# The lower left quarter of a symmetric score matrix from block transposes on VectorE and DMA

## The reference

```
h = layernorm(x) * (1 + ca) + sa              # per batch, 1024 x 256
scores = (h * w_lhs) @ (h * w_rhs).T          # 1024 x 1024
x = x + ga * (softmax(scores, axis=-1) @ h)
h = layernorm(x) * (1 + cb) + sb
x = x + gb * (relu(h @ W1 + b1) @ W2 + b2)    # 256 -> 1024 -> 256
```

## Time and profile before

| | us |
|---|---|
| median of three runs | 720.35 |
| the profiled execution, whole | 725.38 |
| its span | 723.5 |
| TensorE busy | 708.4 (98%) |
| VectorE busy | 562.3 (78%) |
| ScalarE busy | 404.5 (56%) |
| GpSimd busy | 353.8 (49%) |

### The profile page before, as it was taken

How to read it: one execution, slowest core, us unless ns; L and a number is a source line. 1 busy time by engine, 2 the same in 40 slices (tenths; PEclk the granted TensorE clock), 3 DMA queues, 4 the chain that set the end, 5 groups by cost and what they waited for, 6 DMA issues and landing times.

```text
span 723.5 us, 13394 instructions
## 1 busy us (share of the span) xinstructions
PE 708.4 (98%) x4711; PEld 647.2 (89%) x4711; DVE 562.3 (78%) x1041; ACT 404.5 (56%) x565; POOL 353.8 (49%) x394
## 2 busy tenths in 40 slices
PE   8989899999999999999999999999999999999997
PEld 7667789998999989999899989999899998999996
DVE  3578788888889888897898887898888974886521
ACT  2244319842587427872586715874278725665462
POOL 3363336462665245562564526752455624235543
PEclk8889999999999999999999999999999999999999
DMA  8022342213611253122432225112531222011300
GB/s 291 24 82 68 108 117 88 95 59 108 166 49 59 88 170 91 58 84 81 125 87 87 79 78 169 50 58 87 160 101 58 80 84 91 1 37 59 94 32 30
DMA packets 52288, 63.92 MB, mean 88 GB/s; under 512 B 4576, under 2 KB 46624, under 8 KB 52256
## 3 DMA queue, kind: packets, MB, share of 16 engines
q1 hardware_dynamic: 52256, 63.50, 28.7%
HBM read 39.34 MB, written 24.15 MB: 88 GB/s over the span
## 4 chain that ended last, share of the span: by engine, by line
PE 88%; DVE 2%; POOL 0%; issue 0%; DVEq 0%
PE acc L481 8%; PE col L536 8%; PE col L538 8%; PE acc L482 8%; PE col L537 8%; PE acc L487 8%; PE score L597 7%; PE score L600 7%; PE score L596 7%; PE score L521 4%; PE score L522 4%; PE score L523 4%; PE score L527 3%; PE score L579 1%; POOL ln_t L916 0%; DVE score L771 0%
## 5 line engine op out<-in xcount | busy, mean ns | idle before, releaser
L925 POOL TENSOR_TENSOR hid_lo<-hid,hid_hi 128x512 fp32r<-128x512 f32 x128 | 170.4, 1333 | 246.1 <-ACT hid_hi L625 245.3
L621 ACT ACTIVATE hid<-col,b1T 128x512 f32<-128x512 f32 x128 | 87.1, 680 | 113.0 <-PE col L538 107.1
L481 PE MATMUL acc<-W2hi,hid_hi 128*128 128x256 f32 x512 | 127.2, 282 | 0.0
L482 PE MATMUL acc<-W2lo,hid_hi 128*128 128x256 f32 x512 | 125.7, 279 | 0.0
L597 PE MATMUL score<-V,Phi 128*128 128x256 f32 x448 | 109.8, 283 | 0.0
L596 PE MATMUL score<-V,Phi 128*128 128x258 f32 x448 | 109.6, 280 | 0.0
L625 ACT ACTIVATE hid_hi<-hid 128x512 fp32r<-128x512 f32 x128 | 81.0, 633 | 49.2 <-PE acc L487 45.3
L749 DVE TENSOR_SCALAR_CACHE_REDUCE S<-score 128x1024 f32<-128x1024 f32 x64 | 78.0, 1220 | 33.9 <-PE score L527 29.8
L536 PE MATMUL col<-h2hi,W1hi 128*128 128x512 f32 x256 | 103.0, 402 | 0.2 <-DVE h2lo L848 0.2
L538 PE MATMUL col<-h2hi,W1lo 128*128 128x512 f32 x256 | 101.0, 394 | 0.0
L537 PE MATMUL col<-h2lo,W1hi 128*128 128x512 f32 x256 | 100.6, 393 | 0.0
(11 more groups left out here) (106 smaller groups left out, 1366.9 us busy)
## 6 DMA issues: line engine op xcount, KB each, us to landing
block_rows<-blocks SPq DMA_DIRECT2D x30, 512.0 KB, 2.9
blocks<-block_rows SPq DMA_DIRECT2D x120, 128.0 KB, 3.0
x_cur<-x SPq DMA_DIRECT2D x16, 512.0 KB, 3.9
ln_t<-x SPq DMA_DIRECT2D x14, 512.0 KB, 4.8
out<-x_mlp SPq DMA_DIRECT2D x8, 512.0 KB, 3.0
out<-x_mlp SPq DMA_DIRECT2D x16, 256.0 KB, 2.2
W_sb<-W SPq DMA_DIRECT2D x2, 1024.0 KB, 10.1
attn_mod<-mod_rows SPq DMA_DIRECT2D x8, 256.0 KB, 3.5
```

Of the source, the lines that this page charges most:

```text
L481: nc.tensor.matmul(o, hi, W2hi[:, it, :], start=(it == 0 and t % 2 == 0), stop=False, skip_group_check=True)
L482: nc.tensor.matmul(o, hi, W2lo[:, it, :], start=False, stop=False, skip_group_check=True)
L621: nc.scalar.activation(hid[:, n % 2, :], col[n % 2][:], ACT.Relu, bias=b1T[:, n % FT:n % FT + 1]).then_inc(col_read, 1)
L925: G.tensor_tensor(hid_lo[:, n % RING, :], hid[:, n % 2, :], hid_hi[:, n % RING, :].bitcast(F32), ALU.subtract).then_inc(hid_lo_done, 1)
```

## The change

For batches 1 to 7 TensorE no longer makes the lower left quarter (rows 512 to 1023, columns 0 to 511) of the scores. Batch 0 is computed as before.

- SC.4 to SC.7 compute, transpose and copy the right 512 columns only. Of their 4, 5, 6 and 6 transposes 0, 1, 2 and 2 are left.
- ST.0 to ST.3, new on VectorE: the right half of row tile n (128x512) is transposed in 32x32 blocks into `stage`.
- SW.0 and SW.1, new on SyncE's queue: each stores two tiles of `stage` (512 KB) to DRAM. SR.0 and SR.1 load them back in four DMAs of 128 KB each, with the blocks in their new places, into `lower`. `stage` and `lower` lie over the rings `Phi` and `Plo`.
- SB.0 to SB.3 become two subtractions of 512 columns, from `S` and from `lower`.
- MX.0, new on VectorE: the maximum over `lower` (128x2048) per row tile, and a maximum of four columns with `row_max`.
- MB is split: MB.0 (four transposes) can run when row tile 3 is read, MB.1 waits for MX.
- Waits: ScalarE's SM.1 waits until `stage` is stored, VectorE's SM.1 and SM.2 until `lower` is read.
- All lists are in another order. Of those only the loop's start on SyncE is shown in the diff.

```diff
-        AM.0 GA.0- S2.1- XT.0+ X1.0 GB.0 R2.1- SH.0+ XT.1+ RH.0+ O0.0- SH.1+ RH.1+ S2.0 R2.0 X0.0+ O1.0-
+        AM.0 GA.0- S2.1- X1.0 XT.0+ SW.0 R2.1- SR.0 SW.1 SR.1 SH.0+ XT.1+ RH.0+ GB.0 SH.1+ O0.0- RH.1+ S2.0
...
+                    elif kind == "SW":
+                        sp.wait_ge(stage_done, HT * (b - 1) + 2 * n + 2)
+                        sp.dma_start(score_blocks[n], stage[:, n].rearrange("p u v t r -> p (u v t r)")).then_inc(stage_stored, 16)
+                    elif kind == "SR":
+                        sp.wait_ge(stage_stored, 16 * (2 * b + n - 1))
+                        for u in range(Q):
+                            sp.dma_start(lower[u * QP:(u + 1) * QP, n].rearrange("a u v t r -> a u (v t r)"),
+                                         score_blocks[n][:, u * 2 * P:(u + 1) * 2 * P].rearrange("(u a) f -> a u f", a=QP)).then_inc(scores_turned, 16)
...
-                        for lo_col in range(0, ROWS, HR):
+                        left = 0 if n < HT or ph is PH["first"] else HR
+                        for lo_col in range(left, ROWS, HR):
...
-                        for i in range(at // P):
+                        for i in range(left // P, at // P):
...
+                        if ph is PH["first"] or n == 1:
+                            pe.wait_ge(scores_read, T * b + T)
+                        else:
+                            pe.wait_ge(scores_read, T * b + HT)
+                        if ph is not PH["first"] and n == 1:
+                            pe.wait_ge(max_ready, b)
+                        for j in range(n * HT, (n + 1) * HT):
...
-                        V_.tensor_scalar(S[:, n, :], score[n % 2][:], 1.0, None, ALU.mult, ALU.max,
+                        cols = slice(0 if n < HT or ph is PH["first"] else HR, ROWS)
+                        V_.tensor_scalar(S[:, n, cols], score[n % 2][:, cols], 1.0, None, ALU.mult, ALU.max,
...
+                        V_.tensor_tensor(tile[:, 0:HT], tile[:, 0:HT], most.broadcast_to([P, HT, P]), ALU.subtract)
+                        dve.wait_ge(scores_turned, 16 * Q * (2 * b + n // 2 - 1))
+                        V_.tensor_tensor(by_quarter(tile[:, HT:T]), lower[:, n // 2, :, :, n % 2, :].rearrange("p u v r -> p v u r"),
+                                         by_quarter(most.broadcast_to([P, HT, P])), ALU.subtract).then_inc(sub_done, 1)
+                    elif kind == "ST":
+                        dve.wait_ge(scores_read, T * b + n + 1)
+                        V_.transpose(stage[:, n // 2, :, :, n % 2, :], S[:, n, HR:ROWS].rearrange("p (v u r) -> p u v r", v=HT, r=QP)).then_inc(stage_done, 1)
+                    elif kind == "MX":
+                        wait_apart(dve, scores_turned, 16 * Q * 2 * b)
+                        V_.tensor_reduce(left_max[:], lower[:].rearrange("p h u v t r -> p v (h u) (t r)"), AX.XY, ALU.max).then_inc(left_done, 1)
+                        wait_apart(dve, scores_read, T * b + T)
+                        dve.wait_ge(left_done, b)
+                        V_.tensor_tensor(row_max[:, HT:T], row_max[:, HT:T], left_max[:], ALU.max).then_inc(max_ready, 1)
```

More of the change, by code:

```diff
@@ L9 @@
 ACT = mybir.ActivationFunctionType
+AX = mybir.AxisListType
 P = 128
@@ L229, in block_kernel @@
     mod_rows = nc.dram_tensor("mod_rows", [NB, 4, D], F32, kind="Internal").ap()
+    score_blocks = nc.dram_tensor("score_blocks", [2, P, Q * 2 * P], F32, kind="Internal").ap()
     block_rows = nc.dram_tensor("block_rows", [P, D * HT], F32, kind="Internal").ap()
@@ L250, in block_kernel @@
         with nc.sbuf_tensor("W1_sb", [P, DK, FF], F32) as W1_sb, nc.sbuf_tensor("W2_sb", [P, FT, D], F32) as W2_sb:
+            pass
+        with nc.sbuf_tensor("stage", [P, 2, Q, HT, 2, QP], F32) as stage, nc.sbuf_tensor("between", [P, 2, T, P], F32), \
+                nc.sbuf_tensor("lower", [P, 2, Q, HT, 2, QP], F32) as lower:
             pass
@@ L575, in part @@
                     elif kind == "MB":
-                        pe.wait_ge(scores_read, T * b + T)
-                        for j in range(T):
+                        if ph is PH["first"] or n == 1:
[5 more added lines that the diff above has]
+                        for j in range(n * HT, (n + 1) * HT):
                             last = nc.tensor.transpose(max_ps[:, j * P:(j + 1) * P], row_max[:, j:j + 1].broadcast_to([P, P]), ident[:])
-                            if j % HT == HT - 1:
-                                last.then_inc(max_done, 1)
+                        last.then_inc(max_done, 1)
                     elif kind == "AV":
@@ L755, in part @@
                             dve.wait_ge(max_done, 2 * b + n // HT + 1)
-                        most = max_ps[:, n * P:(n + 1) * P].unsqueeze(1).broadcast_to([P, T, P])
-                        V_.tensor_tensor(tile, tile, most, ALU.subtract).then_inc(sub_done, 1)
+                        most = max_ps[:, n * P:(n + 1) * P].unsqueeze(1)
+                        if ph is PH["first"] or n >= HT:
+                            V_.tensor_tensor(tile, tile, most.broadcast_to([P, T, P]), ALU.subtract).then_inc(sub_done, 1)
+                            continue
+                        V_.tensor_tensor(tile[:, 0:HT], tile[:, 0:HT], most.broadcast_to([P, HT, P]), ALU.subtract)
+                        dve.wait_ge(scores_turned, 16 * Q * (2 * b + n // 2 - 1))
+                        by_quarter = lambda ap: ap.rearrange("p v (u r) -> p v u r", u=Q)
+                        V_.tensor_tensor(by_quarter(tile[:, HT:T]), lower[:, n // 2, :, :, n % 2, :].rearrange("p u v r -> p v u r"),
[9 more added lines that the diff above has]
+                        V_.tensor_tensor(row_max[:, HT:T], row_max[:, HT:T], left_max[:], ALU.max).then_inc(max_ready, 1)
                     elif kind == "SM":
+                        if n in (1, 2):
+                            wait_apart(dve, left_done, b)
+                            wait_apart(dve, sub_done, T * b + 2 * n)
                         dve.wait_ge(phi_done, T * (b - 1) + n + 1)
```

99 lines of the change are left out of this document (51 added, 48 removed).

## The result

The changed kernel takes 728.68 us (median of 4 runs, 727.33 to 730.62) where the kernel before, in the same session, takes 720.49: the ratio is 1.0118, with a 95% interval of 1.0092 to 1.0145. The forecast was 710.0 with a range of 706.5 to 717, so it missed in sign. The profiled execution took 729.4 us, with a span of 727.6.

The account below looks back on a forecast made before the run. TensorE was taken to bound the kernel from 82 to 718 us. Median before 720.35, less 12.3 for transposes, plus 0.8 in batch 0, plus 0.15 a batch for small waits, gave 709.9, rounded to 710; range 706.5 to 717.

Parts of the forecast that it names:

- place 1: At the loop's edge, AV.3 to F.0: VectorE needs 20.1 us, TensorE's work 21.0, leaving 0.9 us spare.
- The first rival: VectorE late at the loop's edge, 0.5 to 1.1 us a batch: 712.5 to 717; chance 0.30 including a dear reduction.
- The clause on the port: VectorE and GpSimd share a port, locked by VectorE's two-SBUF-input reads; added instructions with one such input lengthen nothing.
- The transposes: 112 left out of SC.4 to SC.7 in seven batches, 0.110 us each: 12.3 us off TensorE, the ceiling.
- the prices of the added work: VectorE's ST, MX and split SB less halved copies: +2.95 us a batch, 72.5 to 75.4; MX at 2.2.
- bounds of +1.7 and +5.4: Lower and upper limit in us of the work a batch added to VectorE, put at +2.95.
- Place 2: Scores' trip through DRAM after ST.1: 8.0 us, covered by 8.4 us of VectorE work; MB.1 about 6 to spare; cost 0.
- place 3: Row tile 5, SC.6's last transposes behind L1.0's wait for `ln_t`: half a microsecond at most against 0.8 spare; cost 0.
- slower rival: DMA trip holds VectorE at SB.0; over 1.3 us of wait is its sign; 13 us trip ends at 733; chance 0.04.
- The tail: After the last batch, a reordering behind a TensorE that has no gap: 0 us.
- the 0.15 for small waits: Waits shorter than could be resolved, 0.15 us a batch, seven times, added to the sum.
- Batch 0: AV.4 is read later on VectorE, so batch 1's F.0 starts at 82.9: +0.8 us, bounds -0.5 and +2.5.

Follow-up runs that it names:

- e3: Changed kernel with the output store O0.0 ahead of SH.1 on SyncE's queue in the loop: 721.44 us.
- e4: Changed kernel with B2.0 behind XG.1 and SM.6 on VectorE in the loop: 722.91 us.
- e5: Changed kernel with GpSimd's three adds of attn_mod (XC.1 to XC.3) moved ahead in the loop's list: 725.34 us.
- e1: Kernel before, with TensorE leaving out the 16 left transposes of SC.4 to SC.7 in batches 1 to 7; result not computed: 710.97 us.
- e8: Changed kernel with the output store ahead of SH.1 and B2.0 behind XG.1 and SM.6, GpSimd's list untouched: 717.40 us.
- e12: As e8, with MB.1 in batch 1 moved on TensorE from behind F.7 to behind F.8: 714.96 us.
- e6: Changed kernel with output store ahead of SH.1, B2.0 behind XG.1 and SM.6, and GpSimd's adds early: 721.18 us.
- e2: Changed kernel with its lists but without ST, SW, SR and MX, SB.0 to SB.3 as whole subtractions; result not computed: 725.56 us.
- e13: As e8, without ST, SW, SR and MX and with the subtraction whole again; result not computed: 713.59 us.
- e14: As e8, with MX's reduction of `lower` made twice: 729.58 us.
- e7: Loop of the kernel before in its own order with only the change put in, other parts as in the changed kernel: 793.66 us.

## Why the prediction was wrong

**The step that failed is place 1, the loop's edge.** Its sum put VectorE at 20.1 us from the start of AV.3 to the end of T2.0, let it start when TensorE ends AV.3, and gave TensorE 21.0 us to F.0: 0.9 to spare. Measured, VectorE starts 2.2 us after TensorE's end of AV.3 (313.66 against 311.47) and needs 22.2 (to 335.87), 24.4 together. TensorE's own work there is 22.0 us, so 2.4 are missing, and TensorE waits 2.5. Inside, the wait of 1.59 us at B2.0 had been put at nothing and SM.6 at 1.15; and what made VectorE late at the start, the wait of 1.22 us at XG.0 and SM.2 at 3.10, stood ahead of the place where the sum begins and had no term at all.

- *Before AV.3.* XG.0 had been moved ahead of AV.3, and the store that it must wait for behind SH.1. The kernel's lists show both, the SyncE line in the diff the second. The prediction's place 1 began behind them. e3 moves the store: AV.3 starts 0.8 to 0.9 us late instead of 2.2, and 7.2 us come back.
- *Inside.* B2.0 waits for N2.0, which GpSimd can begin only when AV.3's statistics are there: 315.43 on VectorE to 320.86 on GpSimd, 5.4 us. In between VectorE had only TH.0 and SB.7, 3.9 us. That could be foreseen: in the trace of before GpSimd takes from 311.28 to 317.04 for L2.0 and N2.0. No run takes this wait away; e4 shows only that work put in front of it lengthens N2.0 by as much.
- *Long Plo.* SM.2 at 3.10 and SM.6 at 2.32 us, against the 1.15 of the sum. e4 frees SM.6 and gets 5.8 us back; e5 frees SM.2, and AV.3 is 0.2 us late. The first rival named this (712.5 to 717 us, chance 0.30) but priced it at 0.5 to 1.1 us a batch; with the two waits that it did not name it is 2.5.

**The clause on the port.** GpSimd ran two instructions with two inputs beside SM.2 (300.26 to 303.36):

```profile
299.73 1.30 POOL L975 TENSOR_TENSOR hid_lo<-hid,hid_hi 128x512 fp32r<-128x512 f32 x1
300.97 1.30 POOL L1021 TENSOR_TENSOR x_cur<-x_cur,attn_mod 128x512 f32<-128x512 f32 x1
```

With the adds moved, SM.2 took 1.74 us (e5). The added instructions did lengthen nothing (ST 698 ns, the halves of SB 672 and 679; only MX's small companion, 0.20 us in the loop, has two SBUF inputs), by which the rule of the Trainium skill, "SBUF — State Buffer", section "SBUF: two separate sides", was read rightly. But it was applied to the added instructions only. The moved ones are those with two SBUF inputs: the eight Plo of a loop batch went from a mean of 1319 ns to 1593, 2.2 us a batch.

**The transposes** were sized rightly: 12.3 us forecast, 1.8 us a batch and 12.4 in all by e1's trace. One wait and the half clock behind it took 3.7 us back in that execution; whether the like happened in the others, so that the median shows 10.0, is not known. The Trainium skill, "VectorE: DVE Perf Modes", section "The three transpose paths", at 390 ns each was three and a half times too dear here; 0.11 us was measured.

**Right** were the prices of the added work (MX 2.2 against 2.28). VectorE's 75.4 us a batch against 75.30 is in part luck: the sum left every other instruction as it was, and the eight Plo take 2.2 us more than before while Llo, Rlo, V and XG take 2.0 less (11.1 instead of 13.1). (Its bounds of +1.7 and +5.4 leave out the 0.25 of MX's companion; with it they are 1.95 and 5.65.) Place 2 was right in the loop, where the DMA's waits reached TensorE in no batch, and place 3 was right. In batch 1 place 2 was not: SB.0 and SB.2 waited 3.1 us for `lower`, 2.6 of it at once, more than the 1.3 that the prediction named as the sign of its slower rival, and MX was late for MB.1 by 2.08 us, where the prediction, having looked at the loop's list alone, had 6 to spare. By these rows the trip would account for those 2.08; no run takes it away alone. It has no part in the loop's loss. The tail, put at 0, is 0.9 us longer, with a wait of 0.77 for ScalarE's hid. The test "the forecast fails if the period stays above 84" was the right one.

**The sum, put right.** Per loop batch: 84.55 before, 1.8 less for the transposes (82.7, e1), 0.9 more between the matmuls in the new order and at each restart behind a wait (83.6), 2.5 of waits: 86.17. With e8's two edits the 0.9 become 0.5 and the 2.5 become 0.5, and the period is 83.7. Five batches at +1.6 are the loss of 8 us; with e12's third edit the kernel ends 5.7 us below before.

Between e12 and the forecast 5 us remain. From batch 1's F.0 to the end of the span e12 takes 636.3 us and the kernel before 641.4; forecast were 11.3 less, and 5.1 came. Of the 6.2 missing, 4.6 lie in the five loop batches (83.9 on average against 82.8 and the 0.15 for small waits; 0.7 of these 0.9 are the wait at F.0, and the AV matmuls take 23.3 us a batch from start to start against 23.0 in e1), 0.5 in batches 1 and 7, and 1.2 in the tail. Batch 0 came out about 1 us better than forecast. In e6, with SM.2 freed from GpSimd's adds, F.0's last 0.5 us are gone from four of the five loop batches, and the wait for ScalarE's hid costs more than that. A version that frees SM.2 without delaying hid_lo wasn't tried, nor one that takes B2.0's wait away.

## What to carry to other kernels

When a change brings a new order, list for each engine what every moved step waits for, DMA stores and buffer releases too, and follow the wait back through the in-order queue that it stands in; adding up durations from an assumed start proves nothing on an engine that is nearly 90% busy. Before judging the idea, take the added work out and keep the order (e2), and take the removed work out and keep the old order (e1): those two runs said here that the idea was worth 10 to 12 us and the order cost more. But what is taken out or put in moves everything behind it to stand beside other instructions (SM.2 took 1.7 to 4.3 us in these kernels), so read the busy time again, and ask once more in the mended order (e13). Then look at the waits of the bounding engine, follow each to the first instruction in its list that waited itself, and move that one.

## What the runs showed of the hardware

- A 128x1024 subtraction of two SBUF inputs on VectorE took 1.2 us alone and 3.10 beside two of GpSimd's two-input instructions, 1.74 when the adds among these were moved (e5), where another such subtraction, now beside a hid_lo, went from 1.23 to 2.20, and 4.28 beside three of GpSimd's (e14).
- Four 128x256 scale-and-shift instructions on GpSimd (N2.0) took 2.17 us, and 3.87 beside a 128x1024 subtraction of two SBUF inputs on VectorE (e4, e8).
- A transpose of 128x128 in float32 on TensorE took 0.090 to 0.097 us from start to start in a row of four or six. Sixteen left out of a batch gave 1.8 us, 0.11 each, since behind a row of them the distance between the next two matmuls was 0.08 us longer too.
- A reduction of 128x2048 float32 to four columns, over a strided view, took 2.28 us, 1.1 ns a column, as the plain copies did.
- In e7's wait of 13.3 us the granted clock of TensorE fell to half, the lower of its two levels, and the first instructions behind the wait ran at it.
